# Placing the routing steps of a mixture of experts between attention heads: one step a head in the first batch, or one at every second head of the first two

## The reference

```python
x = x + cross_attention(layernorm(x), ctx, Wq, bq, Wk, bk, Wv, bv)    # 77 keys a batch, and each row's own
h = layernorm(x)
q, k, v = split(h @ W_qkv + b_qkv)                # 16 heads of 32
attn_out = softmax(q @ k.T / sqrt(32)) @ v         # 512 x 512 scores a head and batch
gate = softmax(h @ W_gate + b_gate)                # 8 experts
top_g, top_i = top_k(gate, 2)
moe_out = sum over the two chosen experts e of top_g * (h @ W_experts[e] + b_experts[e])
return x + attn_out + moe_out
```

## Time and profile before

| what | value |
|---|---|
| median of 3 runs | 1406.44 us (1406.14 to 1407.71) |
| profiled execution, first to last instruction | 1410.6 us, mean granted TensorE clock 0.962 |
| TensorE matmul busy | 1305.5 us, 93% |
| VectorE busy | 967.5 us, 69%, 2143 instructions |
| ScalarE busy | 903.4 us, 64% |
| POOL busy | 363.8 us, 26% |
| attention stage | some 411 to 1130 us of the span |

### The profile page before, as it was taken

One profiled execution on the slowest core, in us unless ns is written; L12 is line 12 of the kernel. 1 busy time (PEld: TensorE's weight loads), 2 busy tenths in 40 slices (PEclk: granted clock), 3 DMA queues, 4 the chain that ended last, 5 costly groups with the idle time before them and its releaser, 6 DMA issues. The chain is left out here.

```text
span 1410.6 us, 27655 instructions
## 1 busy us (share of the span) xinstructions
PE 1305.5 (93%) x7744; PEld 994.7 (71%) x7745; DVE 967.5 (69%) x2143; ACT 903.4 (64%) x1888; POOL 363.8 (26%) x572
## 2 busy tenths in 40 slices
PE   4998999999888899999999999999988779999996
PEld 4967888888666567776777776777764358777775
DVE  4256888888678888888888888888876524433332
ACT  4123545444358799999999999999987723333332
POOL 0002222222200011312102131110010047777765
PEclk9998999999899999999999999999996789999998
DMA  5006777776665257564545745556479377867763
GB/s 163 1 1 228 265 268 264 251 266 246 231 164 150 38 135 161 134 165 85 145 128 138 188 84 123 143 144 164 104 166 309 131 191 140 146 124 134 139 129 52
DMA packets 113387, 219.83 MB, mean 156 GB/s; under 512 B 28489, under 2 KB 36809, under 8 KB 111155
## 3 DMA queue, kind: packets, MB, share of 16 engines
q1 hardware_dynamic: 84064, 173.47, 40.9%
q0 software_dynamic: 26624, 42.04, 17.3%
q10 hardware_dynamic: 2643, 3.65, 0.8%
HBM read 86.82 MB, written 77.73 MB: 117 GB/s over the span
## 5 line engine op out<-in xcount | busy, mean ns | idle before, releaser
L225 PE MATMUL banks<-parts 128*128 128x512 f32 (+6 forms) x1108 | 443.0, 400 | 32.7 <-DVE parts L1334 7.4
L227 PE MATMUL banks<-parts 128*128 128x512 f32 (+6 forms) x1108 | 423.5, 382 | 0.0
L226 PE MATMUL banks<-parts 128*128 128x512 f32 (+6 forms) x1108 | 422.9, 382 | 0.0
L1549 DVE TENSOR_REDUCE plain<-banks 128x1 f32<-128x512 f32 x512 | 339.5, 688 | 82.9 <-PE banks L1053 69.8
L774 ACT ACTIVATE banks<-banks,plain 128x512 f32<-128x512 f32 x512 | 346.2, 683 | 15.4 <-DVE plain L1549 15.1
L781 ACT ACTIVATE plain<-banks 128x1024 f32<-128x1024 f32 x256 | 266.9, 1043 | 39.6 <-PE banks L1075 38.4
L225 PEld LDWEIGHTS banks<-parts 128*128 128x128 f32 (+1 forms) x1108 | 214.2, 193 | 85.4 <-issue 24.2
L227 PEld LDWEIGHTS banks<-parts 128*128 128x128 f32 (+1 forms) x1108 | 213.0, 192 | 40.8
L226 PEld LDWEIGHTS banks<-parts 128*128 128x128 f32 (+1 forms) x1108 | 214.4, 194 | 30.8
L1075 PE MATMUL banks<-parts 104*128 104x512 f32 x512 | 179.8, 433 | 6.2 <-ACT plain L781 4.7
L1053 PE MATMUL banks<-parts 96*128 96x512 f32 x512 | 184.9, 413 | 0.7 <-ACT banks L774 0.3
(11 more groups left out here) (180 smaller groups left out, 1506.8 us busy)
## 6 DMA issues: line engine op xcount, KB each, us to landing
parts<-parts SPq DMA_DIRECT2D x384, 128.0 KB, 2.4
parts<-h_turned SPq DMA_DIRECT2D x46, 512.0 KB, 6.5
experts_split<-parts SPq DMA_DIRECT2D x32, 512.0 KB, 4.1
h_turned<-parts SPq DMA_DIRECT2D x32, 512.0 KB, 2.9
parts<-experts_split SPq DMA_DIRECT2D x8, 2048.0 KB, 9.8
plain<-in_x_dram SPq DMA_DIRECT2D x32, 256.0 KB, 4.1
plain<-in_L_ffn_W_experts_dram SPq DMA_DIRECT2D x32, 256.0 KB, 4.1
out_dram<-plain SPq DMA_DIRECT2D x32, 256.0 KB, 2.8
```

Of the source, the lines that this page charges most:

```text
L225: pe.matmul(out, stat[0], mov[0], start=first, stop=False)
L226: pe.matmul(out, stat[0], mov[1], start=False, stop=False)
L227: return pe.matmul(out, stat[1], mov[0], start=False, stop=last)
L1549: dve.tensor_reduce(nmx[:, k, t:t + 1], bank[SB[t]][:], AX.X, ALU.max, negate=True).then_inc(q["f_max"], 1)
```

## The change

The fourteen steps of LATER stand at heads 0, 2, 4, ... 26, counted through the batches 0 and 1, where they stood at heads 0 to 8 and 10 to 14 of batch 0. For this batch 1 is taken out of the loop on VectorE, and on SP too, whose wait for r_zero and write of the list now stand behind batch 1. On POOL attended(0, 1) and attended(1, 0) come ahead of the wait for r_zero; then come four place in a row, attended(1, 1), and three place and two attended for each of the batches 2 to 5. TensorE and ScalarE run the same code.

```diff
@@ sync: -479 +479
             batch(0, True, False)
+            batch(1, False, False)
             sp.wait_ge(q["r_zero"], 1)
             sp.dma_start(slot_dram.rearrange("(p i) c -> p i c", p=P), lst).then_inc(q["r_zeroed"], 16)
-            with sp.Fori(1, B - 1) as b:
+            with sp.Fori(2, B - 1) as b:
                 batch(b, False, False)
             batch(B - 1, False, True)
@@ gpsimd: -557 +558
             attended(0, 0)
+            attended(0, 1)
+            attended(1, 0)
 
             pool.wait_ge(q["r_zero"], 1)
@@ -573 +576
-            PER = (2 * B - 1) // (B - 3)
-            assert 1 + PER * (B - 3) == 2 * B
-            place(0)
-            attended(0, 1)
-            with pool.Fori(1, B - 2) as b:
-                place(PER * b - PER + 1)
+            PER = 3
+            AHEAD = 2 * B - PER * (B - 4)
+            assert AHEAD > 0
+            for m in range(AHEAD):
+                place(m)
+            attended(1, 1)
+            with pool.Fori(2, B - 2) as b:
+                place(PER * b + AHEAD - 2 * PER)
                 attended(b, 0)
                 for m in range(1, PER):
-                    place(PER * b - PER + 1 + m)
+                    place(PER * b + AHEAD - 2 * PER + m)
                 attended(b, 1)
@@ vector: -1539 +1544
-            LATER = {0: over_tiles_1, 1: over_tiles_2, 2: over_tiles_3, 3: first_blocks_1, 4: first_blocks_2, 5: rank_places, 6: places, 7: first_records,
-                     8: second_records, 10: block_experts, 11: block_places, 12: block_firsts, 13: block_order, 14: list_zero}
+            LATER = {2 * n: step for n, step in enumerate((
+                over_tiles_1, over_tiles_2, over_tiles_3, first_blocks_1, first_blocks_2, rank_places, places, first_records,
+                second_records, block_experts, block_places, block_firsts, block_order, list_zero))}
@@ -1594 +1600
-                    if first and k in LATER:
-                        LATER[k]()
+                    if isinstance(b, int) and b * NH + k in LATER:
+                        LATER[b * NH + k]()
@@ -1603 +1609
             batch(0, True, False)
-            with dve.Fori(1, B - 1) as b:
+            batch(1, False, False)
+            with dve.Fori(2, B - 1) as b:
                 batch(b, False, False)
             batch(B - 1, False, True)
```

## The result

The changed kernel takes 1432.26 us (median of 4 runs, 1425.63 to 1438.36) where the kernel before takes 1407.08 beside it (4 runs, 1406.14 to 1411.02): a ratio of 1.0181, 95% interval 1.0147 to 1.0215. It is slower, as forecast, but by 25 us and not by 4, far outside the range. (The ratios of this document are those of the record, which are not the quotients of the two medians; the two differ by up to 0.16%.) The profiled execution has a span of 1434.6 us, 24.0 more than that of before.

The account below looks back on a forecast made before the run. TensorE was taken to set attention's pace, with routing steps on VectorE delaying it. VectorE +2.1, clock +1.6 and records and DMA +0.2 summed to +3.9 us on the 1406.44 median: 1410.3 us, range 1405.8 to 1413.4.

Parts of the forecast that it names:

- The step that failed: VectorE's and SP's batch 1 as straight code: taken as 0 us, bounds -0.5 and +0.5.
- The rule of the margins: Attention heads: a VectorE step costs its length less its place's margin: 1.34 us whole, 0 begun, 0.34 to 0.44 ended.
- The sum for VectorE: Routing steps in batches 0 and 1: +2.6 us from new places, -0.55 at the opening, together +2.1 us.
- The clock: TensorE, batch 1: one clock fall behind block_places' 3.6 us idle stretch, charged +1.6 us, bounds 0 and 3.2.
- +3.5 for the two batches: Batches 0 and 1 together: 187.4 us forecast where they took 183.9.
- POOL, SP and the records: Later list zeroing and record DMAs: no late waits, 30 us to spare; DMA hits on VectorE copies net +0.2 us.
- Rival 5: POOL's run of 16 records is slow, making attended(1, 1) late; at twice 1.97 us near 10 us late, 1420; chance 0.04.
- Rival 1: Spreading works: 0.40 us absorbed per head over 27 heads, whatever the place; -4.8 us, 1401.6; chance 0.11.
- Rival 2: TensorE's clock holds or its fall is covered: +2.3 us, 1408.7; chance 0.14.
- rival 3: Nothing moves, since a later wait takes up the difference: 1406.4 us; chance 0.06.
- rival 4: Margins gone as well, VectorE still behind from the step two heads before: +6.3 us, 1412.7; chance 0.07.
- The sign: Whole kernel: slower, +3.9 us; chances slower 0.64, same 0.26, faster 0.10.

Follow-up runs that it names:

- e9: Changed kernel with routing steps back at their old heads and 12 idle VectorE instructions ahead of the loop (start 842); 1405.08 us, ratio 1.0003 to the kernel before.
- e1: Kernel before with 29 idle VectorE instructions ahead of the attention loop, moving its start from 673 to 702; 1424.76 us, ratio 1.0152.
- e2: Changed kernel with 12 idle VectorE instructions ahead of the attention loop, moving its start from 830 to 842; 1407.80 us, ratio 1.0036 to the kernel before.
- e4: Changed kernel with routing steps cut into single instructions, dealt to heads 0 to 31 by margin, loop at 855; 1396.21 us, ratio 0.9958 to the kernel before.
- e6: Changed kernel, steps dealt by margin over 48 heads, batch 2 also straight code, list zeroed earlier, loop at 1004; 1389.88 us, ratio 0.9920 to the kernel before.
- e5: Changed kernel with 12 idle instructions ahead of the loop and block_places split over heads 4 and 5 of batch 1; 1407.12 us, ratio 1.0033 to the kernel before.
- e10: Kernel before with 24 idle VectorE instructions ahead of the attention loop, moving its start to 697; 1431.45 us in a single run.

## Why the prediction was wrong, point by point

- **The step that failed** is the last of the working: "VectorE's and SP's batch 1 become straight code ... I take 0, with bounds of -0.5 and +0.5." Straight code costs nothing in itself (e9), nor does the loop's turn as it stood; but the 157 instructions moved the loop to a start at which every turn fetches code, and that cost 19.5 us of the 24 that the profiled execution is longer. I had read the loop's turns in the trace of before and took that as a property of the loop. It is one of the loop at start 673. e1 and e2 show it from both sides. The trace of before had a hint, the instruction queue silent during the loop; what it could not give is the length of the stall.
- **The rule of the margins** was right. By head, what batches 0 and 1 lost in after against the undisturbed pattern (behind the slash the forecast): in batch 0 heads 5 0.55/0.56, 7 0.81/0.71, 9 1.41/1.40, 11 1.95/1.72, 13 0.90/0.89, 15 0.96/0.92; in batch 1 heads 1 1.36/1.27, 3 2.02/2.04, 5 3.59/3.61, 7 1.26/1.10, 9 0.72/0.70, 11 0.28/0.20. The sum for VectorE was +2.1; these terms came out within 0.23 us each, and 0.7 us above the forecast together. e4 and e6, worked out from the same margins, came within 0.2 us of the expected batches.
- **The clock** fell once, where I said, but the term was mis-sized: head 6 of batch 1 is 3.1 us longer, not 1.6. I had taken the length of the fall from the earlier trace rows, 3.4 us after a 2.15 us wait; after 3.45 us of waiting the lower level lasts from some 535.4 us to 542. These 1.5 us are most of the 1.9 between my +3.5 for the two batches and the +5.4 of after. That the clock fell is in part luck: I had argued from a 1.90 us wait that left it alone and longer ones that didn't, and e1 has 2.91 us that left it alone.
- **POOL, SP and the records** cost nothing, as said: batch 2 of e2 takes 85.25 us with the whole run of records in it. Rival 5 (records slow) is out with their spacing of 1.97 us. Its own sum was off too: at twice that spacing attended(1, 1) would come 7 us late (597 and 63 and 7, against 660), not 10.
- **What no row of mine showed:** that the 2.26 us stand before 1047.00 let the clock fall. The earlier trace rows has only the stand; in the trace the clock behind it is 0.64 over 1047 to 1050 us, so the reading holds.
- **Rival 1** (spreading works by itself) is out: e2 spreads over 27 heads and loses 5.2 us. Rival 2 (no cost of the clock) is out by clock 0.96 in batch 1, rival 3 (nothing moves) by e2's interval, and rival 4 (margins gone as well) by the heads above.
- Without the stall the forecast would have been near: +3.9 for +5.2 in the trace, and e2's ratio of 1.0036 puts it at +5.1 us (3.0 to 7.2), with its middle inside the range. The sign was right for a reason worth a fifth of the loss.

## What to carry to other kernels

When an edit changes how many instructions stand ahead of a loop (the runs show it for VectorE alone), read whether the instruction queues move packets while the loop runs, before and after: a dozen idle instructions were worth 20 us here, more than anything that was scheduled. Filler work on an engine that another one waits for is priced by the place where it goes, not by how thinly it is spread: measure the margin of each place and cut the filler to fit. And sum by batch periods rather than whole times where a later stage differs between runs by more than the effect.

## What the runs showed of the hardware that I had not expected

- A loop of 266 VectorE instructions stalls at each turn, 2.2 and 1.7 us in after, when it starts at rests 57 or 62 (of 128), and not at 33, 53, 67, 71, 74, 76, 87 or 108. The second stall comes two instructions into the loop at rest 62 and seven at rest 57. Each turn then moves five packets of some 8 KB. The rest of the turn's cost in after, 1.6 to 2.9 us in head 1, goes for the most part with TensorE's clock after 2.2 to 2.7 us of standing; where the clock held (e1's first two turns) it is 0.45 us.
- The length of TensorE's wait doesn't settle the clock: it fell after 1.88 us in e5 and 1.85 us in e10, but not after 1.90 us in before, and not after 2.46 and 2.91 us in e1, where it fell after 3.06. After 3.4 us it fell in each profile that has such a wait, after and e2, and stayed low longer than after 2.15 us.
